# First and third expert weights kept, fetched and awaited in two halves by columns

## The reference

```
logits = xt @ gate_w.T + gate_b;  scores = softmax(logits);  top_w, top_i = top_k(scores, 2)
expert(e): h = silu(xt @ w1[e].T + b1[e]) * (xt @ w3[e].T + b3[e]);  return h @ w2[e].T + b2[e]
y = sum over e of expert(e) * gate_dense[:, e]
z = silu(xt @ ws1.T + bs1) * (xt @ ws3.T + bs3) @ ws2.T + bs2
x = x + layernorm(y + z)
```

## Time and profile before

| | us |
|---|---|
| median of three runs | 1211.28 |
| the profiled execution | 1204.67 |
| its span, first to last instruction | 1202.9 |
| expert stage within the span | about 755 to 1118 |
| PE busy over the span | 1003.4 (83%) |
| DVE busy | 844.9 (70%) |
| POOL busy | 794.4 (66%) |
| ACT busy | 569.5 (47%) |

### The profile page before, as it was taken

How to read it: one execution, slowest core, us unless ns; L and a number is a source line. 1 busy time by engine, 2 the same in 40 slices (tenths; PEclk the granted TensorE clock), 3 DMA queues, 4 the chain that set the end, 5 groups by cost and what they waited for, 6 DMA issues and landing times. The chain is left out here.

```text
span 1202.9 us, 22915 instructions
## 1 busy us (share of the span) xinstructions
PE 1003.4 (83%) x6344; PEld 885.7 (74%) x6344; DVE 844.9 (70%) x2227; ACT 569.5 (47%) x1013; POOL 794.4 (66%) x790
## 2 busy tenths in 40 slices
PE   0667799999999999999997775879999999989562
PEld 0456578777877787778776764879999999989341
DVE  3577798778877887787878323646777767766486
ACT  3333654566446644664555233424444444434265
POOL 2234777887788777877887533256776666666498
PEclk9877999999999999999999777889999999999655
DMA  4233332453245324532443117678768787787698
GB/s 133 66 92 110 97 101 85 154 155 101 81 149 157 103 79 147 159 110 77 141 145 97 54 53 235 182 165 221 116 118 183 149 195 168 164 196 182 187 365 317
DMA packets 105204, 174.05 MB, mean 145 GB/s; under 512 B 13229, under 2 KB 75336, under 8 KB 102856
## 3 DMA queue, kind: packets, MB, share of 16 engines
q1 hardware_dynamic: 73960, 121.09, 31.9%
q0 software_dynamic: 26592, 35.67, 16.4%
q10 hardware_dynamic: 4608, 16.78, 3.8%
HBM read 173.53 MB, written 78.21 MB: 209 GB/s over the span
## 5 line engine op out<-in xcount | busy, mean ns | idle before, releaser
L1495 POOL DMA_INDIRECT sum_y<-e_y,e_row_at x142 | 222.6, 1567 | 43.5 <-issue 39.1
L1329 PE MATMUL e_h_ps<-e_z_hi,e_w 128*128 128x256 f32 x1136 | 217.8, 286 | 20.9 <-DMA e_w<-w_split 10.9
L1329 PEld LDWEIGHTS e_h_ps<-e_z_hi,e_w 128*128 128x128 f32 x1136 | 182.8, 193 | 23.7 <-issue 14.9
L1152 POOL DMA_INDIRECT slots_x<-f_xf,f_at x128 | 140.3, 1096 | 32.4 <-issue 32.2
L1329 PE MATMUL e_h_ps<-e_z_lo,e_w 128*128 128x256 f32 x568 | 161.3, 284 | 0.0
L1371 ACT ACTIVATE e_act_h<-e_h_ps,e_w 128x256 f32<-128x256 f32 x142 | 67.4, 475 | 192.2 <-PE e_h_ps L1329 170.9
L615 PE MATMUL f_h_ps<-f_f_hi,f_w_hi 128*128 128x512 f32 x256 | 108.9, 426 | 27.7 <-DVE f_h L909 23.8
L1345 PE MATMUL e_y_ps<-e_w,e_h_hi 128*128 128x256 f32 x568 | 118.4, 292 | 1.1 <-DVE e_h_lo L1417 1.1
L1410 DVE SCALAR_TENSOR_TENSOR e_h<-e_h_ps,e_w,e_act_h 128x256 f32<-128x256 f32 x142 | 68.0, 483 | 65.7 <-ACT e_act_h L1371 57.8
L876 DVE RECIPROCAL f_den<-f_den 128x256 f32<-128x256 f32 x64 | 111.6, 1746 | 1.1
L1329 PEld LDWEIGHTS e_h_ps<-e_z_lo,e_w 128*128 128x128 f32 x568 | 109.3, 192 | 0.0
(11 more groups left out here) (222 smaller groups left out, 2968.7 us busy)
## 6 DMA issues: line engine op xcount, KB each, us to landing
e_w<-w_split SPq DMA_DIRECT2D x71, 1026.0 KB
e_w<-w_split ACTq DMA_DIRECT2D x71, 512.0 KB
e_x_in<-slots_x SPq DMA_DIRECT2D x71, 260.0 KB
f_x_in<-x SPq DMA_DIRECT2D x16, 512.0 KB, 5.1
f_x_res<-x SPq DMA_DIRECT2D x16, 512.0 KB, 6.0
x_dram<-f_x SPq DMA_DIRECT2D x16, 512.0 KB, 7.0
sum_y<-f_y SPq DMA_DIRECT2D x32, 256.0 KB, 2.9
c_acc<-sum_y SPq DMA_DIRECT2D x16, 512.0 KB, 7.5
```

What stands on the lines that cost most here:

```text
L1152: pool.indirect_dma_start(out=slots_x[:, :], out_offset=bass.IndirectOffsetOnAxis(ap=at[p][:, j, k:k + 1], axis=0), in_=xf[p][:, j, :], in ...
L1329: last = pe.matmul(h_ps[q][:, which, :], w13(p, part)[:, which, c, q * P:(q + 1) * P], z[p % 2][:, c, :], start=(n == 0), stop=(n == 5))
L1495: pool.indirect_dma_start(out=dst[:, :], out_offset=bass.IndirectOffsetOnAxis(ap=row_at[p][:, j:j + 1], axis=0), in_=y[p][:, j, :], in_off ...
```

## The change

The buffer of w1 and w3 becomes two, one for each q: `w13_all[p][0]` with the columns that `inner(·, 0)` reads (1024 words, 512 KB), and `w13_all[p][1]` with those of `inner(·, 1)` and the four bias columns (1028 words, 514 KB). `w_split` is laid out so that each half is contiguous in a partition's row; for that the host orders the columns of w1 and w3 otherwise, and the first pass stores an even step's part in four DMAs instead of two. SP calls `load_w` twice per tile, each with its own reading of `tile_expert` and `tile_new` and its own wait. PE waits for a half before each inner product. ACT waits for the second half before the first silu, since the biases lie there.

```diff
@@ first_pass, SP
                         if half == 0:
-                            at = i * (W_ALL // 2) + low * W13
-                            sp.dma_start(w_split[:, bass.ds(at, HALF_W)], words).then_inc(w_stored, 32)
+                            at = i * (W_ALL // 2) + low * PART
+                            sp.dma_start(w_split[:, bass.ds(at, PART)], words[:, 0:PART]).then_inc(w_stored, 16)
+                            sp.dma_start(w_split[:, bass.ds(at + 2 * PART, HALF_W - PART)], words[:, PART:])\
+                                .then_inc(w_stored, 16)
                         else:
                             at = (i - 1) * (W_ALL // 2)
-                            sp.dma_start(w_split[:, bass.ds(at + low * W13 + HALF_W, W13 - HALF_W)],
+                            sp.dma_start(w_split[:, bass.ds(at + (1 + low) * PART + HALF_W, W13 - HALF_W)],
                                          words[:, 0:W13 - HALF_W]).then_inc(w_stored, 16)
@@ expert_tiles
+    PART = W13 // parts
-        w13_all = [sb(f"w13_{p}", [P, 2 * W13 + 2 * parts], F32R) for p in range(2)]
+        w13_all = [[sb(f"w13_{q}{p}", [P, 2 * PART + (2 * parts if q == parts - 1 else 0)], F32R) for q in range(parts)]
+                   for p in range(2)]
-        w13_loaded = [sem(f"w13_loaded{p}") for p in range(2)]
+        w13_loaded = [[sem(f"w13_loaded{q}{p}") for q in range(parts)] for p in range(2)]
@@ expert_tiles, SP
-                    load_w(sp, n, w13_all[par % 2], 0, w13_loaded[par % 2], (h13_done, (n - 1) * parts),
+                    p = par % 2
+                    load_w(sp, n, w13_all[p][0], 0, w13_loaded[p][0], (h13_done, (n - 2) * parts + 1))
+                    load_w(sp, n, w13_all[p][1], 2 * PART, w13_loaded[p][1], (h13_done, (n - 1) * parts),
                            (h_ready, (n - 1) * parts))
@@ expert_tiles, PE
                 if q == 0:
                     pe.wait_ge(zlo_ready, s + 1)
-                    pe.wait_ge(w13_loaded[p % 2], landed(s, p % 2))
+                pe.wait_ge(w13_loaded[p % 2][q], landed(s, p % 2))
@@ expert_tiles, ACT
                 act.wait_ge(h13_done, s * parts + q + 1)
+                if q == 0:
+                    act.wait_ge(w13_loaded[p % 2][parts - 1], landed(s, p % 2))
@@ kernel
-    ffn = [chunked(w[e]).reshape(128, -1) for e in range(w1.shape[0]) for w in (w1, w3, w2)]
+    def by_parts(a, b):
+
+        both = _np.stack([chunked(a), chunked(b)], 1)
+        return both.reshape(128, 2, both.shape[2], -1, 128).transpose(0, 3, 1, 2, 4).reshape(128, -1)
+
+    ffn = [w for e in range(w1.shape[0]) for w in (by_parts(w1[e], w3[e]), chunked(w2[e]).reshape(128, -1))]
```

More of the change, by code:

```diff
@@ L203, in first_pass @@
     W13, W2 = 4 * HALF_W // 3, 2 * HALF_W // 3
+    PART = W13 // 2
+    assert W13 - HALF_W < PART < HALF_W
     assert SEQS == 2 * E and W_ALL % 2 == 0
@@ L1254, in words, with w13 @@
             return ap.bitcast(F32)
-        def w13(p, part):
-            return w13_all[p % 2][:, part * W13:(part + 1) * W13].rearrange("p (a b n) -> p a b n", a=2, b=CC)
+        def w13(p, q, part):
+            return w13_all[p % 2][q][:, part * PART:(part + 1) * PART].rearrange("p (a b n) -> p a b n", a=2, b=CC)
         def w2(p, part):
@@ L1262, in bias @@
         def bias(p, which, q):
-            at = 2 * W13 + which * parts + q
-            return words(w13_all[p % 2][:, at:at + 1])
+            at = 2 * PART + which * parts + q
+            return words(w13_all[p % 2][parts - 1][:, at:at + 1])
         def load_w(eng, n, to, at, done, *waits):
@@ L1328, in inner @@
                         for part, z in ((HI, z_hi), (HI, z_lo), (LO, z_hi)):
-                            last = pe.matmul(h_ps[q][:, which, :], w13(p, part)[:, which, c, q * P:(q + 1) * P],
+                            last = pe.matmul(h_ps[q][:, which, :], w13(p, q, part)[:, which, c, :],
                                              z[p % 2][:, c, :], start=(n == 0), stop=(n == 5))
```

## The result

The changed kernel takes 1223.49 us (median of 9 runs, 1220.67 to 1226.05), the kernel before 1209.82 us beside it (9 runs, 1206.38 to 1217.13). The ratio is 1.0105, 95% interval 1.0087 to 1.0123, which is 12.7 us of 1209.82; the two medians differ by 13.7 us. The change is slower clear of noise, and its time lies half a us above the 1208 to 1223 that I gave the main case. I had expected +4.3 us. The profiled execution of after took 1224.7 us, that of before 1204.67. So the pair of traces shows 20 us of difference, 6 more than the medians: the traced execution of before is 5.1 us under its median and under all nine runs, that of after 1.2 us over its own.

A forecast was written before the change was run, and what follows sets the result against it. The prediction took PE to bound the expert stage, with idle time between tiles to gain. Terms of +7.8, -4 and +0.5 us gave +4.3 on a median of 1211.28, so 1215.6 us; main case 1208 to 1223, overall 1200 to 1229.

The forecast's parts named there:

- the main case: Whole kernel: SP falls behind and some scatter waits shorten; median 1215.6 us, range 1208 to 1223, chance 0.50.
- SP's lag per tile: SP's queue, expert stage: second load_w takes 1.7 us against 1.36 to spare, so 0.34 us lag per tile (0.30 to 0.43).
- gain of the halves: PE at each switch of expert: the first half lands earlier, the second is needed 1.4 us later; 1.3 us gained per switch.
- first pass: Before the expert stage: 16 more DMA issues, 7.8 us of SP, ahead of SP's existing waits; cost 0.
- start of the stage: Expert stage's first tiles: two more load_w before the third input's issue delay it; +0.5 us (0 to 1.5).
- scattered rows: DVE's waits for sum_y rows near 790 and 800 us: halves let scatters in sooner, 2 us each; -4 us.
- What the lag costs: PE at switches of expert: each us of lag costs one, less 1.3 us gain per switch; +7.8 us in all.
- the rival of the scatters: Early expert stage: both DVE waits for scattered rows vanish, and the low clock behind them; 1207 us, chance 0.15.
- my own signs: Expected in the trace, among others: first half issued 1.7 us after the input, second 1.7 us after the first, neither waiting.
- SP becomes the bound outright: Expert stage: load_w costs 1.86 us or more, lag 0.5 us per tile, PE waits nearly every tile; 1227 us, chance 0.20.
- SP keeps up: Expert stage: added instructions cost under 1.36 us per tile, no lag builds, only gains remain; 1198 us, chance 0.15.
- The scatters get free: Early expert stage: DVE's two waits, 8.1 us, and the low clock behind them vanish; 1207 us, chance 0.15.

The follow-up runs named there:

- e3_late: `e1_shared` with the first half waiting for what the whole waited for before the change; 1203.03 us, ratio 0.994 to the kernel before.
- e1_shared: The changed kernel with SP reading tile_expert and tile_new once per tile for both halves; 1201.06 us, ratio 0.9925 to the kernel before.

## Why the prediction was wrong

The cause was the one foretold, SP's second pair of readings, and the sum was too small by 8 to 9 us in the medians. The terms, against the pair of traces. The first three lines are the lag and the gain, the others add up to the whole; each is read between the starts of two tiles:

| step | predicted | measured |
|---|---|---|
| SP's lag per tile | 0.34 us | 5.03 - 4.68 = 0.35 us (0.40 in the four tiles above) |
| lag at the first half of tile 33 | 6.1 us | 928.40 - 920.01 = 8.4 us |
| gain of the halves at tile 33 | +1.3 us | second half: 9.0 - 1.4 = 7.6 us for the 6.5 of the whole, a loss of 1.1 us |
| first pass, to the first turn | 0 | -0.95 us |
| start of the stage, to tile 2 | +0.5 us | +2.05 us |
| scattered rows, tiles 2 to 10 | -4 us | -2.3 us |
| tiles 10 to 14 | 0 | +1.4 us |
| waits from tile 14 on | with the lag, +7.8 us in all | +10.9 us |
| low clock at the switches | not in the sum | +9.6 us (estimate) |
| behind the last tile's start | 0 | -0.6 us |
| sum | +4.3 us | +20.0 us |

The first pass can't be told from its spread: over the ten traces of this case the first turn starts between 749.0 and 751.1 us.

**The step that failed is "What the lag costs".** It counted each us of lag as one of PE and left the clock out, although had the price of it: after a wait of 4 us tile 8 took 2.5 us more than its 4.68. I had that number only in the rival of the scatters, as something that could be gained. At tile 33 PE waits 3.19 and 2.53 us, and the two matmul groups between and behind them run at half clock, which makes the 3.4 us read above; in the four stretches it is 9.6. By switch, the sum had +4.8, +0.7, +1.8, +0.4 and +0.1 us for tiles 33, 41, 52, 59 and 65; behind each of them the changed kernel is +10.9, +3.9, +3.0, -0.6 and +3.2 us further back, of which 3.4, 1.7, 3.1, 0 and 1.5 are the clock. That the clock costs this is read from the windows, not from an experiment: no run here keeps the waits and changes only the clock.

**In the same step, the gain of the halves.** I assumed the second half to land when the whole does now, and gave it 1.4 us of slack. But it is issued 1.65 us after the first, which my own signs had at 1.7: the slack was spent before it set out. Without w2's transfers it is in use 8.2 us after the first half's issue, so the count is 8.2 - 1.4 = 6.8 us for the 6.5 of the whole, and with them 7.6.

**The lag's start.** I let the lag begin at 0. SP comes into the stretch late in both kernels: the input of tile 12's step goes out 4.5 us after that tile's start (826.38) in before and 4.4 us (826.01) in after, where the place in the even stretch is 918.06 - 915.56 = 2.5 us. The kernel before takes these 2 us back with its spare time, the changed one has none; 6.7 us come on top in its 19 tiles. First before, then after:

```profile
830.92 0.34 SPq L1283 DMA_DIRECT2D e_x_in<-slots_x  x1
918.06 0.25 SPq L1283 DMA_DIRECT2D e_x_in<-slots_x  x1
```

```profile
830.45 0.34 SPq L1289 DMA_DIRECT2D e_x_in<-slots_x  x1
926.09 0.34 SPq L1289 DMA_DIRECT2D e_x_in<-slots_x  x1
```

**The start of the stage** was outside its range of 0 to 1.5 us. The sum looked at the third input only; one added `load_w` stands before the second as well. Its issue follows the first input's by 2.96 us before and by 4.75 after, and PE's second turn waits for it:

```profile
754.84 1.11 PE L1313 MATMUL e_turn_ps<-eye,e_x_in 128*128 128x128 f32 x4 [3.53 <-DMA e_x_in<-slots_x]
```

```profile
755.84 1.12 PE L1321 MATMUL e_turn_ps<-eye,e_x_in 128*128 128x128 f32 x4 [5.48 <-DMA e_x_in<-slots_x]
```

From the first turn to the second it is 6.6 us in the trace of after and 6.2 in that of the changed kernel without w2, and 4.2 to 4.9 in the eight others.

**What was right.** The permission to fetch earlier is worth nothing in this order: `e3_late` and `e1_shared` can't be told apart. SP's spare time of 1.36 us is real: a second issue without its readings keeps 8.7 us of waits for `e_gate`, and readings alone give the loss back. Waits added on PE's queue cost nothing that shows: from tile 14 to tile 21 every tile of after takes 4.68 us.

**The rivals.** "SP becomes the bound outright" had the right side and its sign in the trace: from tile 22 to tile 32 nearly every tile takes longer than 4.68 us, with short waits of PE from 875 us on. But its condition did not hold: the lag was 0.35 to 0.40 us per tile and not 0.5. The 2 us that SP brought along let it fall behind PE's need sooner. "SP keeps up" fell, and `e1_shared` is near the kernel that it described: it is 9 us faster, and not 13. "The scatters get free" fell for the most part. PE's idle time for DVE went from 8.4 us in 3 waits to 1.9, but waits for weights of 2.01 and 1.51 us took its place at tile 8, and DVE's second wait for rows got longer. First after, then the second wait before:

```profile
794.37 0.16 DVE L1452 TENSOR_TENSOR e_first_too<-e_own,e_x_in 128x2 f32<-128x2 f32 x1 [3.05 <-DMA sum_y<-e_y,e_row_at]
806.42 0.16 DVE L1452 TENSOR_TENSOR e_first_too<-e_own,e_x_in 128x2 f32<-128x2 f32 x1 [8.36 <-DMA sum_y<-e_y,e_row_at]
```

```profile
807.66 0.16 DVE L1442 TENSOR_TENSOR e_first_too<-e_own,e_x_in 128x2 f32<-128x2 f32 x1 [7.40 <-DMA sum_y<-e_y,e_row_at]
```

The first became shorter (6.11 us in the earlier trace rows), the second longer. The Trainium skill ("DMA: Bandwidth & Descriptors", Queues, rings and completion order) has each DMA engine drain a whole packet of one queue before it switches; a smaller load would then hold up a scatter for less time. The first wait agrees, the second speaks against it as all that counts here.

The other rule that I cited from that page of the Trainium skill, 2.0 us plus bytes over 436 GB/s, is a fit to DMAs that GpSimd issues (Anatomy of one DMA), while these loads are SP's. It gives 3.2 us for a half. At tile 33 the first half was in use 3.55 us after its issue, near the rule; the second, issued at 930.05 and in use at 937.40, 7.35 us, far from it.

**Open.** How the fetch of w2 makes the lag dearer, since at tile 33 the second half is nearly as late without it. Why one execution of a kernel differs from the next by several us, so that the pair of traces is 20 us apart and the medians 13.7. The trace of `e1_shared` (1203.02 us) is in the same way 1.7 us below that of before, and its median 8.8 us below.

## What to carry to other kernels

An engine that only issues DMAs has no busy time on the page, and can be the bound all the same. Before adding an issue to its queue, take its spare time from its own waits (here 1.36 us per tile) and the price from the gap between two of its issues (here 1.71 us, nearly all of it reading numbers into registers). Ask too whether the queue comes into the stretch late, since without spare time it stays late. Share such readings between issues, and put the issue whose condition holds first ahead of the one that waits longer: the same halves are 1% slower with two readings, 0.7% faster with one, and 1.5% faster with one and in the other order. And where a wait of PE grows to 2 us and more, a low clock may follow it and nearly double the price.

## What the runs showed of the hardware that was not expected

In four places of the changed kernel a low clock followed waits of PE of 2 to 3 us at a switch: with those of 3.19 and 2.53 us at tile 33 it lasted 10.2 us. The kernel before, whose longest wait for weights was 2.2 us, has none from 813 us on. But the length of one wait does not decide it: in the kernel with two readings added PE waits 2.60, 2.92 and 2.84 us at tiles 41, 53 and 59, and the granted clock stays at 1.00 around each:

```profile
1031.57 0.39 PE L1331 MATMUL e_h_ps<-e_z_hi,e_w 128*128 128x256 f32 x1 [2.92 <-DMA e_w<-w_split]
```

```profile
1029.00:1040.00 11.00, 8.43 (x72) 8.44 (x73) 5.70 (x19) 3.14 (x7) 4.54 (x5) 1.00 0.80 188
```

A conditional DMA that moves no data took SP 73 to 84 ns of issue at the median, but its readings and its address 1.6 us.
